# A Mamba scan whose sums over states are accumulated transposed, and one more product on GpSimd

## What is computed

```python
delta = softplus(dt @ dt_proj_w.T + dt_proj_b)                 # (L=224, D_INNER=1024)
deltaA = exp(delta[..., None] * A)                             # (L, 1024, 16 states)
deltaBu = delta[..., None] * Bm[:, :, None, :] * xc[..., None]
h = deltaA * h + deltaBu                                       # scan over L, per channel and state
y = einsum('bdn,bn->bd', h, c)                                 # sum over the 16 states
y = (y + xc * Dp) * silu(z)
out = x + y @ out_proj_w.T
```

## Time and profile before

| | |
|---|---|
| median of 3 runs | 2643.19 us (2641.14 to 2646.1) |
| span of the profiled execution, first to last instruction | 2642.7 us |
| the 16 steps in that execution | 60.65 to 1893.50 us |
| busy in the whole span: PE, DVE, ACT, POOL | 92%, 79%, 66%, 68% |
| mean granted clock of PE | 0.955 of full speed |

### The profile page before, as it was taken

The page is one execution under the profiler, slowest core; times in us unless marked ns, Lnnn a source line. Parts: engine busy times, 40 slices in busy tenths (PEclk is TensorE's granted clock), DMA queues, the critical chain, the costliest instruction groups (busy, mean ns, idle before and its releaser), DMA issues.

```text
span 2642.7 us, 33255 instructions
## 1 busy us (share of the span) xinstructions
PE 2432.5 (92%) x11291; PEld 2063.5 (78%) x11291; DVE 2085.4 (79%) x2288; ACT 1751.7 (66%) x4011; POOL 1786.3 (68%) x1044
## 2 busy tenths in 40 slices
PE   6788999999999999999999999996869999999997
PEld 6676877878778787877878787775648999999996
DVE  4898999999999999999999999998633444444452
ACT  5667888878888888888888888886543333333331
POOL 1989999999999999999999999999510100000100
PEclk9899999999999999999999999998869999999998
DMA  6042202212021220202112020220142343333420
GB/s 210 8 129 68 84 15 84 72 35 88 19 84 41 66 88 12 91 15 84 51 56 88 12 91 15 77 71 28 59 141 96 130 142 115 112 122 132 141 77 18
DMA packets 90852, 202.62 MB, mean 77 GB/s; under 512 B 7948, under 2 KB 16794, under 8 KB 90702
## 3 DMA queue, kind: packets, MB, share of 16 engines
q1 hardware_dynamic: 81486, 179.21, 20.9%
q0 software_dynamic: 5120, 14.21, 1.7%
q10 hardware_dynamic: 4096, 7.34, 0.9%
HBM read 171.32 MB, written 29.95 MB: 76 GB/s over the span
## 4 chain that ended last, share of the span: by engine, by line
PE 44%; POOL 39%; DVE 8%; issue 6%; DMA 2%; ACT 1%; POOLq 0%; SPq 0%; DVEq 0%; ACTq 0%
POOL arena L969 23%; PE work L1605 12%; PE ring L1605 11%; PE y L1586 8%; POOL arena L974 6%; PE work L1394 5%; POOL arena L980 3%; DVE ring L1261 3%; PE work L1433 2%; POOL arena L901 2%; POOL arena L899 2%; POOL arena L897 2%; DVE arena L1104 1%; DVE arena L1270 1%; POOL expert_rows L930 1%
## 5 line engine op out<-in xcount | busy, mean ns | idle before, releaser
L969 POOL TENSOR_TENSOR arena<-arena 128x896 f32<-128x896 f32 x512 | 1058.0, 2088 | 64.0 <-PE y L1586 55.5
L817 ACT ACTIVATE ring<-arena,small 128x224 f32<-128x224 f32 x2048 | 794.7, 436 | 154.8 <-DVE arena L1270 121.2
L1586 PE MATMUL y<-arena,cst_sb 128*128 128x224 f32 x3584 | 774.9, 368 | 101.0 <-POOL arena L980 69.5
L1261 DVE TENSOR_TENSOR_SCAN ring<-ring,arena 128x896 f32<-128x896 f32 x400 | 809.3, 2023 | 61.5 <-POOL arena L969 41.6
L1586 PEld LDWEIGHTS y<-arena,cst_sb 128*128 128x128 f32 x3584 | 695.7, 198 | 173.9 <-POOL arena L980 78.0
L993 POOL DMA_INDIRECT out<-res,ids x32 | 46.8, 1461 | 640.2 <-DVE mst L1318 542.1
L1270 DVE TENSOR_TENSOR arena<-ring,arena 128x896 f32<-128x896 f32 x400 | 433.4, 1083 | 6.0
L1394 PE MATMUL work<-arena 128*128 128x224 f32 x2000 | 426.3, 371 | 11.0 <-DVE arena L1059 6.0
L1394 PEld LDWEIGHTS work<-arena 128*128 128x128 f32 x2000 | 399.1, 202 | 24.1 <-DVE arena L1104 8.6
L1333 DVE SCALAR_TENSOR_TENSOR hidden_lo<-work,hidden_hi 128x448 fp32r<-128x448 f32 x128 | 79.9, 624 | 346.2 <-ACT hidden_hi L867 346.2
L867 ACT ACTIVATE hidden_hi<-work 128x448 fp32r<-128x448 f32 x128 | 69.7, 544 | 370.6 <-PE work L1605 370.6
(11 more groups left out here) (208 smaller groups left out, 3308.3 us busy)
## 6 DMA issues: line engine op xcount, KB each, us to landing
weights<-in_w SPq DMA_DIRECT2D x64, 1024.0 KB, 7.3
arena<-bc_rows SPq DMA_DIRECT2D x128, 448.0 KB, 4.4
arena<-in_ctx SPq DMA_DIRECT2D x16, 896.0 KB, 5.7
expert_rows<-x2e SPq DMA_DIRECT2D x1, 7224.0 KB, 29.7
xrow<-expert_rows SPq DMA_DIRECT2D x8, 903.0 KB, 11.4
arena<-in_xT SPq DMA_DIRECT2D x16, 448.0 KB, 6.4
arena<-in_x SPq DMA_DIRECT2D x16, 448.0 KB, 3.7
out<-arena ACTq DMA_DIRECT2D x32, 224.0 KB, 2.3
```

The source lines that it names most:

```text
L817: last = nc.scalar.activation(decays[s % 2][:, i * L:(i + 1) * L], delta[:, k, :], ACT.Exp, scale=a_neg[:, n:n + 1])
L969: nc.gpsimd.tensor_tensor(u[:, u_of[s]], dx[:, k:k + 1, :].to_broadcast([P, QN, L]), bc[:, 0, q * QN:(q + 1) * QN, :], ALU.mult).then_inc( ...
L1261: nc.vector.tensor_tensor_scan(states, h, u_flat[:, u_of[s], :], 0.0, ALU.mult, ALU.add).then_inc(scan_done, 1)
L1586: last = nc.tensor.matmul(o, ident, u[:, u_of[s], i, :], start=False, stop=(q == Q - 1 and i == QN - 1), skip_group_check=True)
```

## The change

- PE no longer multiplies the product by the identity. For each of the 32 slots it takes the product tile itself as weights, half a state (112 tokens) at a time, and streams the identity in transpose mode: 8 instructions for a slot, accumulated in `yt_bank` as 112 tokens x 128 channels, four such areas for a pair.
- When the eight slots of a pair are done, ACT copies the bank to SBUF (`sums_copied`, jobs `yt0` to `yt3`, 112 x 512), and PE transposes it back with four instructions on top of xc * Dp in the one remaining `y_bank` (`turn_back`, jobs `back0` to `back3`). The gate waits for that.
- POOL's additions are gone (`ADDED`); `POOLED` has slot 29 as well, so POOL makes 8 products and DVE 24.
- `u_of` goes round all five buffers throughout. The tables move a few jobs. The scratch of software DMAs is set to 8192 bytes.

```diff
-    u_of = [s % 5 if s < 20 else s % 4 for s in range(SLOTS)]
+    u_of = lambda b, s: (b * SLOTS + s) % UB
...
+        yt_sb = sb("yt_sb", [H, 4 * P])
...
+        yt_bank, y_bank = yb
...
+                 "back0": 8.5, "back1": 16.5, "back2": 24.5, "back3": 0.5,
...
-                  "drop1": 6, "sq0": 7, "tap3": 8, "sq1": 9, "skip1": 9.01, "exp": 11, "silu": 11.01, "hx0": 12, "xp": 14,
-                  "skip2": 15, "sp0": 16, "t0": 17, "sp1": 18, "z0": 19, "depool": 21, "z1": 23, "hx1": 23.01, "z2": 24,
-                  "t1": 24.01, "sp2": 25, "skip3": 26, "z3": 27, "square": 27.01, "sp3": 28, "logs": 30, "skip0": 31}
+                  "drop1": 6, "skip0": 6.01, "sq0": 7, "tap3": 8, "sq1": 9.01, "skip1": 14.01, "exp": 11, "silu": 11.01, "hx0": 12, "xp": 14,
+                  "skip2": 22, "sp0": 16, "t0": 16.5, "sp1": 18, "z0": 19, "depool": 21, "z1": 23, "hx1": 23.01, "z2": 24,
+                  "t1": 24.01, "sp2": 25.01, "skip3": 29, "z3": 27, "square": 27.01, "sp3": 28, "logs": 30, "yt0": 9, "yt1": 17, "yt2": 25, "yt3": 1.01}
...
-        POOLED = tuple(range(1, SLOTS - Q, 4))
+        POOLED = tuple(range(1, SLOTS, 4))
         MADE = SLOTS - len(POOLED)
-        ADDED = (5, 9, 13, 17)
...
             def skip_columns(step, par, j):
-                if isinstance(step, int) and step == 0 and j < 2:
-                    act.wait_ge(y_plain, j + 1)
-                need(act, y_done, step * PAIRS + (j - 1))
+                if isinstance(step, int) and step == 0 and j == 0:
+                    act.wait_ge(y_plain, 1)
+                need(act, y_done, step * PAIRS + j)
                 if j == 0:
                     act.wait_ge(xc_ready, step + 1)
                 for i in range(2):
                     k = 2 * j + i
-                    last = nc.scalar.activation(yb[j % 2][:, i * L:(i + 1) * L], xc[:, par, k, :], ACT.Copy, scale=d_skip[:, k:k + 1])
+                    last = nc.scalar.activation(y_bank[:, i * L:(i + 1) * L], xc[:, par, k, :], ACT.Copy, scale=d_skip[:, k:k + 1])
                 last.then_inc(skip_ready, 1)
+
+            def sums_copied(step, j):
+
+                act.wait_ge(sum_done, step * SLOTS + 2 * Q * (j + 1))
+                need(act, y_back, step * PAIRS + j)
+                nc.scalar.activation(yt_sb[:], yt_bank[0:H, 0:4 * P], ACT.Copy).then_inc(yt_copied, 1)
...
-                def first_skip():
-                    yield "skip0"
-                    skip_columns(nxt, 1 - par, 0)
+                def sums():
+                    for j in range(PAIRS - 1):
+                        yield f"yt{j}"
+                        sums_copied(b, j)
+                def last_sums():
+                    yield f"yt{PAIRS - 1}"
+                    sums_copied(e, PAIRS - 1)
...
-                    last = max((p for p in range(s) if u_of[p] == u_of[s]), default=max(p for p in range(SLOTS) if u_of[p] == u_of[s]) - SLOTS)
-                    need(pool, sum_done, b * SLOTS + (last + 1))
+                    need(pool, sum_done, b * SLOTS + s - UB + 1)
                     if isinstance(b, int) and b == 0 and s == 0:
                         pool.wait_ge(s_rows, 16)
                     if s < Q:
                         pool.wait_ge(bc_loaded[q], b * 32 + 32)
                     if s % (2 * Q) == 0:
                         pool.wait_ge(delta_done, b * 4 + (s // (2 * Q) + 1))
-                    nc.gpsimd.tensor_tensor(u[:, u_of[s]], dx[:, k:k + 1, :].to_broadcast([P, QN, L]),
+                    nc.gpsimd.tensor_tensor(u[:, u_of(b, s)], dx[:, k:k + 1, :].to_broadcast([P, QN, L]),
                                             bc[:, 0, q * QN:(q + 1) * QN, :], ALU.mult).then_inc(u_ready, 1)
                     if s - 2 in POOLED:
-                        q = (s - 2) % Q
+                        q, states = (s - 2) % Q, u[:, u_of(b, s - 2)]
                         pool.wait_ge(scan_done, b * SLOTS + (s - 1))
-                        nc.gpsimd.tensor_tensor(u[:, u_of[s - 2]], u[:, u_of[s - 2]], bc[:, 1, q * QN:(q + 1) * QN, :], ALU.mult
-                                                ).then_inc(pooled_ready if s - 2 not in ADDED else multiplied, 1)
-                    if s - 2 in ADDED:
-                        pool.wait_ge(multiplied, b * len(ADDED) + (ADDED.index(s - 2) + 1))
-                        apart(pool)
-                        product_made(pool, b, s - 3)
-                        nc.gpsimd.tensor_tensor(u[:, u_of[s - 2]], u[:, u_of[s - 2]], u[:, u_of[s - 3]], ALU.add
-                                                ).then_inc(pooled_ready, 1)
+                        nc.gpsimd.tensor_tensor(states, states, bc[:, 1, q * QN:(q + 1) * QN, :], ALU.mult).then_inc(pooled_ready, 1)
...
-                dve.wait_ge(sum_done, b * SLOTS + 2 * Q * (j + 1))
+                dve.wait_ge(y_back, b * PAIRS + (j + 1))
...
-                nc.vector.tensor_tensor(v, v, yb[j % 2][:, 0:2 * L].rearrange("p (k l) -> p k l", k=2), ALU.mult).then_inc(y_done, 1)
+                nc.vector.tensor_tensor(v, v, y_bank[:, 0:2 * L].rearrange("p (k l) -> p k l", k=2), ALU.mult).then_inc(y_done, 1)
...
+            def turn_back(step, j):
+                pe.wait_ge(yt_copied, step * PAIRS + (j + 1))
+                apart(pe)
+                pe.wait_ge(skip_ready, step * PAIRS + (j + 1))
+                for i in range(2):
+                    for h in range(2):
+                        o = i * L + h * H
+                        last = nc.tensor.matmul(y_bank[:, o:o + H], yt_sb[:, (2 * i + h) * P:(2 * i + h + 1) * P], ident[0:H, 0:H],
+                                                is_transpose=True, start=False, stop=(i == 1 and h == 1), skip_group_check=True)
+                last.then_inc(y_back, 1)
...
-                    o = yb[(k // 2) % 2][:, (k % 2) * L:(k % 2 + 1) * L]
-                    if q == 0:
-                        if k % 2 == 0:
-                            pe.wait_ge(skip_ready, b * PAIRS + (k // 2 + 1))
-                            apart(pe)
-                    if s + 1 in ADDED:
-                        return
+                    if s % (2 * Q) == 0:
+                        need(pe, yt_copied, b * PAIRS + k // 2)
+                        apart(pe)
                     product_made(pe, b, s)
                     for i in range(QN):
-                        last = nc.tensor.matmul(o, ident, u[:, u_of[s], i, :], start=False, stop=(q == Q - 1 and i == QN - 1),
-                                                skip_group_check=True)
-                    last.then_inc(sum_done, 2 if s in ADDED else 1)
+                        for h in range(2):
+                            o = (2 * (k % 2) + h) * P
+                            last = nc.tensor.matmul(yt_bank[0:H, o:o + P], u[:, u_of(b, s), i, h * H:(h + 1) * H], ident, is_transpose=True,
+                                                    start=(s % (2 * Q) == 0 and i == 0 and h == 0),
+                                                    stop=(s % (2 * Q) == 2 * Q - 1 and i == QN - 1 and h == 1), skip_group_check=True)
+                    last.then_inc(sum_done, 1)
...
+    nc = bacc.Bacc("TRN2", target_bir_lowering=False, num_devices=1, dynamic_dma_scratch_size=8192)
```

More of the change, by code:

```diff
@@ L800, in side @@
                     (gate_inputs, pro), (residuals, epi), (context, epi), (depool, epi), (next_rows, pre), (logarithms, pre or pro),
-                    (weights, first), (skips, scan), (first_skip, pro)) if there))
+                    (weights, first), (skips, scan), (sums, scan), (last_sums, epi)) if there))
             def body(b, par):
@@ L1523, in plain @@
                         apart(pe)
-                        nc.tensor.matmul(yb[j][:, 0:2 * L], ident, w_in[:, 0, 0:2 * L], start=True, stop=True).then_inc(y_plain, 1)
+                    nc.tensor.matmul(y_bank[:, 0:2 * L], ident, w_in[:, 0, 0:2 * L], start=True, stop=True).then_inc(y_plain, 1)
                 def steps():
@@ L1562, in context, with turned_back, last_turned_back @@
                         yield from cross(b, h)
+                def turned_back():
+                    for j in range(PAIRS - 1):
+                        yield f"back{j}"
+                        turn_back(b, j)
+                def last_turned_back():
+                    yield f"back{PAIRS - 1}"
+                    turn_back(e, PAIRS - 1)
                 def next_rows():
@@ L1570, in side @@
                     (inputs, pro), (gate_inputs, pro), (steps, pro), (routing, tail), (outputs, epi), (patches, epi),
-                    (context, epi), (next_rows, pre), (tokens, isinstance(b, int) and b == -1), (plain, isinstance(b, int) and b == -1)) if there))
+                    (context, epi), (next_rows, pre), (turned_back, scan), (last_turned_back, epi), (tokens, isinstance(b, int) and b == -1), (plain, isinstance(b, int) and b == -1)) if there))
             def body(b, par):
@@ L1734 @@
     }
-    nc = bacc.Bacc("TRN2", target_bir_lowering=False, num_devices=1)
```

(1 more changed line is left out.)

20 lines of the change are left out of this document (10 added, 10 removed), and 8 rows, old and new, of the table DVE_AT.

## The result

The changed kernel takes 2723.02 us (median of 4 runs, 2715.94 to 2726.2) against 2644.58 for the kernel before on the same chip (4 runs): ratio 1.0301, 95% interval 1.0283 to 1.032. It is 3% slower; the forecast was 1.6% faster, and the time lies above its range. The span of the profiled execution is 2720.9 us. The first expert matmul starts at 2043.84 instead of 1963.43, and the experts take 677.1 instead of 679.3 us, so the whole loss of 80 us lies in the steps.

A forecast was written before the change was run, and what follows sets the result against it. DVE, PE and POOL bound a step within 1% of each other; DVE alone would afterwards. Fourteen steps give -24 us, the first -10, the last -8: 2643 - 42 = 2601, stated as 2600, range 2585 to 2615.

The forecast's parts named there:

- the terms of the work: Busy time a step: PE 92.8 us at full clock (0.86 a slot's sums), DVE 108.2, ACT 97.1, POOL 101.5.
- DVE is the engine with the most work: In a full step DVE becomes the bound at 108.2 us, 6.7 over POOL and 15 over PE.
- the one on idle time: DVE's idle in a full step: 5.1 + 1.3 at its end - 2.0 of waits for POOL or `z0` = 4.4 us.
- The second failed step: ACT's four added copies, about 0.6 us each, 2.4 a step; their cost to DVE was counted at nothing.
- chain of a pair: Sums, copy, transposes back, gate, next skip through one bank: about 0.9 + 0.6 + 0.6 us of work; counted at nothing.
- The sign that I named for being wrong: On DVE: waiting for decays right behind `yt1` or `yt2` would show the forecast wrong; no size given.
- The tables leave three to four slots: Between a pair's last sum and its gate: 9 to 12 us of room for copy and transposes back.
- First and last steps: First step 103.3 us, a gain of 10; last step 111.6, a gain of 8; the drain changes under 1.
- The eighth product: End of a step: with slot 29's product on POOL, the product DVE saves (1.00 us) is given back whole.
- slower, by PE's clock: PE's clock falls in the steps; at 0.76, if transposes aren't seen as activity, 122 us a step, 2750 in all; chance 0.13.
- forecast: 2.6 for the two: Where one step passes to the next, DVE's idle time grows from 1.27 to about 2.6 us.

The follow-up runs named there:

- run 1: Changed kernel with PE's `tx0`, `tx1` and `rt` moved ahead of the sums of slot 4: 2696.22 us, 1.0195 of the kernel before.
- run 4: Changed kernel with POOL's four additions back and PE leaving out slots 4, 8, 12 and 16: 2693.53 us, 1.0189 of the kernel before.
- run 9: Kernel before, with PE only waiting for the products of the slots it leaves out: 2656.95 us, 1.0037.
- run 10: Kernel before, without POOL's additions, PE summing all 32 slots in the old form: 2675.04 us, 1.0119.
- run 13: Changed kernel with ACT's copy cut to 8 columns, every place and wait kept: 2727.33 us, 1.0319 of the kernel before.
- run 14: The kernel of run 6 with ACT's copy cut to 8 columns: 2641.29 us, 0.9989 of the kernel before.
- run 5: Changed kernel with the edit of run 1, and `yt1` moved from slot 17 to 18.01: 2666.68 us, 1.0097 of the kernel before.
- run 6: The kernel of run 5 with `yt0` also moved, from slot 9 to 10.01: 2637.97 us, 0.9978 of the kernel before.
- run 7: Changed kernel with the edit of run 1, and `sp0` and `corr0` one slot sooner: 2649.68 us, 1.0037 of the kernel before.
- run 8: Changed kernel with the product of slot 29 back on DVE, 7 products on POOL: 2729.54 us, 1.0337 of the kernel before.
- run 11: Changed kernel with the edits of run 1, run 5, run 6 and run 7 together: 2643.75 us, 0.9992 of the kernel before.
- run 12: The kernel of run 11 with `yt2` also moved, from slot 25 to 26.01: 2640.99 us, 0.9994 of the kernel before.

## Why the prediction was wrong

**Right: the terms of the work.** Eight transposes take 1.04 us and sixteen 1.91, from PE's timeline of the changed kernel (the second full step shown above):

```profile
934.17 1.91 PE L1613 MATMUL y<-cst_sb,arena 128*112 128x128 f32 x16
...
937.63 1.04 PE L1613 MATMUL y<-cst_sb,arena 128*112 128x128 f32 x8
```

That is 0.87 a slot against 0.86, and a transpose that accumulates costs no more than one that doesn't. A copy takes 0.60, as estimated. DVE's and POOL's work are within 0.9. POOL is busy 102.4 and not 101.5 because I took the 0.18 us of idle time before each addition off its busy time as well, 0.7 in all.

**Right: DVE is the engine with the most work**, and POOL's lateness goes. But this was a statement on loads, and the loads did not set the time.

**The step that failed** is the one on idle time: "Waits for late POOL or for `z0` are about 2.0 of it ...: PE won't be behind, and POOL has 6.7 to spare", so 4.4 of idle a step. It is 12.5, the mean 121.1 less 108.6. I took PE's load, 92.8, as the answer to whether PE would be late. PE is late at `tx0` and at slot 15 while it has nothing to do (3.68 and 4.68 us idle), because its stream is in order and the instruction at its head waits for DVE. The prediction looked for who is full, not for what the re-instated sums of slot 4 are queued ahead of and those of slot 15 behind; the chain product 4, sums 4, `tx0`, decays can be read from the tables and from the idle times of before. Runs 1, 4, 9 and 10 show it: moved around, 27 us; slot 4 left out again, 29 with the other three slots; the waits alone put into the old kernel, 12; waits and work there, 30. The second place could be seen in the kernel before, too. There `dt1` waited for `corr0`, from PE's timeline:

```profile
1039.76 1.02 PE L1405 MATMUL work<-dbl,w_dt_sb 33*128 33x224 f32 x4 [1.61 <-DVE arena L1112]
```

Behind this wait the clock was 0.51 and ACT waited 3.97 us for `z0`. The prediction put that down to a PE with too much work; PE had been waiting just before.

**The second failed step** is the copies: "`yt0`, `yt1` and `yt2` stand where a skip was taken away nearby ... I count them at nothing". I weighed their 0.6 us each, and that is indeed next to nothing (runs 13 and 14). The prediction's chain of a pair gave the sums 0.9 us of work and no wait. The sign that I named for being wrong, DVE waiting for decays right behind `yt1` or `yt2`, came: 3.01 and 0.76. What they bring is a wait for PE in the stream of the engine that makes decays just in time. The two ring tiles give ACT a lead of one slot, about 3 us, so a copy that waits 5.40 delays DVE by 3.01. Runs 5 and 6 took 30 and 29 us off by moving `yt1` and `yt0` one slot; run 7 took 47 off by ending the wait at its source instead. "The tables leave three to four slots" was about the way from the copy to the gate; what mattered was the way from the last sum to the copy, and there `dt1` stood.

**First and last steps.** The first takes 109.77, against 103.3 forecast and 113.42 before; the last two with the drain are 0.8 longer than before, against a forecast gain of 10. The same waits stand there too: DVE waits 2.99 us for decays behind `yt1` in the first step, and 3.64, 3.01 and 3.27 from 1741.50 on.

**The eighth product.** I said it is given back whole at the end of the step, and run 8 agrees: steps of the same kind are as long with it as without, within some 0.2 us (a first one of 123.8 apart), and the 6 us between the two programs are the three more long steps, 12 us, less 6 ahead of the full steps. POOL did wait for the scan of slot 29 as described, 0.35 us before L987 at 1012.05, and DVE then 0.81 to 0.84 for the next `u`.

**The rival "slower, by PE's clock" has a part in it, but not as I priced it.** The clock in full steps is 0.90 to 0.94; I had estimated 0.91, and 0.76 if transposes were not seen as activity. PE at 0.91 needs 102 us, under DVE's 108.2, and I left it at that. What I didn't ask is where in the step the clock falls: behind PE's wait at slot 4, on the way to the decays. The long steps cost 22 us more than as many short ones, of the 80; that the two steps compared above differ in the clock behind the same wait, and in nothing ahead of it, is read from the trace; no run sets the clock alone. Four stretches of the changed kernel, with the columns of the earlier trace rows:

```profile
915.90:917.80 1.90, 1.90 (x17) 1.66 (x15) 1.90 (x7) 1.69 (x5) 1.67 (x4) 1.00 0.00 0
802.24:803.30 1.06, 1.06 (x10) 1.06 (x11) 1.06 (x1) 0.00 (x0) 1.06 (x1) 1.00 0.00 0
921.50:923.40 1.90, 1.90 (x9) 1.90 (x10) 1.87 (x1) 0.00 (x0) 1.90 (x1) 0.50 0.00 0
970.10:976.30 6.20, 6.20 (x25) 5.67 (x25) 2.88 (x9) 4.16 (x10) 4.12 (x2) 0.64 0.00 0
```

Sixteen transposes in a row ran at 1.00, the 2.4 GHz level, after 3.1 us of work without a pause. (So they do stand sixteen in a row; the prediction had no more than a slot's eight.) In the long step eight ran at 0.50, 1.2 GHz, and took 1.95 instead of 1.04, right after PE had waited 3.68 us for DVE. In the short step the same eight, after the same wait, ran at 1.00, and the clock fell only later, from about 807 to 811. What decides between the two is open. Run 6, which has the same transposes and shorter waits, has 0.93 and takes 2638 us. The Trainium skill ("TensorE: Matmul & The Clock Gate", Part 4: PE-mode transpose) says that the full clock doesn't engage for transpose-mode work; mixed with ordinary matmuls as here, the trace doesn't agree: 1.00 in the first two stretches. A long stretch of transposes alone was not tried.

**Why not 2600 even without the three waits.** Run 6 has steps of 115.4 (282.25 to 1667.55), 2.8 more than forecast. Its DVE still waits 36.0 us for decays in those nine and a half steps, where the kernel before waited 16.1. The remaining places of the first step shown are 1.71 and 1.06 where it takes over from the step before (forecast: 2.6 for the two), 1.20 at `z0`, where ACT waits 2.72 for PE, and 0.89, 0.75, 0.62 and 0.52 elsewhere. Runs 11 and 12 went at some of them without a gain: the time came back at the next. What share is the fallen clock (0.93 against 0.97) after each wait and what share is the tables' order as a whole is open. That the removed POOL work could buy more in another order is neither shown nor excluded.
